# Layer-1 attention, local rounds: the window is kept by a multiplication on VectorE in place of mask matmuls on TensorE

## The reference

```
def local_gqa_attn(x, wq, wk, wv, wo):
    q, k, v = split_heads(x @ wq, 16), split_heads(x @ wk, 4), split_heads(x @ wv, 4)
    q, k = qk_norm(rope(q, BASE_L)), qk_norm(rope(k, BASE_L))
    diff = i[:, None] - i[None, :]
    mask = (diff >= 0) & (diff < 32)
    return merge_heads(sdpa(q, k, v, mask)) @ wo
```

## Time and profile before

| | us |
|---|---|
| median of 3 runs (lowest, highest) | 2619.33 (2613.45, 2625.76) |
| profiled execution | 2615.01 |
| its span | 2613.3 |
| busy: TensorE, VectorE, ScalarE, GpSimd | 2304.5, 1548.6, 1233.7, 953.9 |
| mean granted TensorE clock | 0.933 |

### The profile page before, as it was taken

The page is one execution under the profiler, slowest core; times in us unless marked ns, Lnnn a source line. Parts: engine busy times, 40 slices in busy tenths (PEclk is TensorE's granted clock), DMA queues, the critical chain, the costliest instruction groups (busy, mean ns, idle before and its releaser), DMA issues. The chain is left out here.

```text
span 2613.3 us, 41691 instructions
## 1 busy us (share of the span) xinstructions
PE 2304.5 (88%) x15308; PEld 1392.4 (53%) x15308; DVE 1548.6 (59%) x3383; ACT 1233.7 (47%) x1733; POOL 953.9 (37%) x925
## 2 busy tenths in 40 slices
PE   5999999999999999756999995699999989937586
PEld 2555565556555655445888883334344444524464
DVE  4676757766777577543666667445555445356534
ACT  2555536553655454312333331577877655613241
POOL 0777757775777577610000002223223211000001
PEclk9999999999999999965999997699999988968798
DMA  2000000000000000020000000000000000020001
GB/s 70 1 1 1 1 1 1 1 1 1 1 1 1 1 1 1 1 61 1 0 0 0 0 1 6 1 1 1 1 1 1 1 1 1 2 75 0 0 1 32
DMA packets 35462, 18.03 MB, mean 7 GB/s; under 512 B 15323, under 2 KB 33125, under 8 KB 35301
## 3 DMA queue, kind: packets, MB, share of 16 engines
q1 hardware_dynamic: 35300, 15.86, 2.4%
HBM read 13.76 MB, written 2.10 MB: 6 GB/s over the span
## 5 line engine op out<-in xcount | busy, mean ns | idle before, releaser
L311 POOL TENSOR_TENSOR a_first<-a_first,a_ring 128x512 f32<-128x512 f32 (+3 forms) x352 | 559.9, 1591 | 141.9 <-ACT a_ring L556 106.6
L1576 ACT ACTIVATE g_probsT<-g_s_ps 128x1024 f32<-128x1024 f32 (+2 forms) x448 | 381.8, 868 | 150.3 <-PE g_s_ps L1460 86.6
L556 ACT ACTIVATE a_ring<-a_st 128x768 f32<-128x768 f32 (+1 forms) x256 | 234.8, 917 | 262.8 <-PE a_st L463 262.8
L478 PE MATMUL a_o_ps<-a_ring,a_v 128*64 128x512 f32 (+3 forms) x1280 | 249.2, 485 | 3.2 <-POOL a_ring L293 2.2
L1485 PE MATMUL g_o_ps<-g_probsT,g_values 128*32 128x512 f32 (+5 forms) x2688 | 231.8, 423 | 20.9 <-ACT g_probsT L1576 16.8
L645 DVE RECIPROCAL a_row_inv<-a_row_inv 128x512 f32<-128x512 f32 x64 | 213.7, 3341 | 16.8 <-ACT a_row_inv L544 16.8
L1045 ACT ACTIVATE m_silu<-m_up,m_bias 128x512 f32<-128x512 f32 x160 | 110.1, 688 | 238.8 <-PE m_up L1012 238.8
L1012 PE MATMUL m_up<-m_xT_hi,m_w_hl 128*128 x640 | 211.9, 402 | 7.1 <-DVE m_glu L1061 4.3
L623 DVE TENSOR_REDUCE a_part_max<-a_mx 128x2 f32<-128x1024 f32 x128 | 156.5, 1223 | 103.1 <-PE a_mx L434 99.6
L1460 PE MATMUL g_s_ps<-g_qT,g_kT 64*128 64x512 f32 (+3 forms) x896 | 208.0, 463 | 10.3 <-ACT g_probsT L1576 9.1
L1343 POOL TENSOR_SCALAR_AFFINE_SELECT g_probsT<-g_probsT 128x512 f32<-128x512 f32 x128 | 88.2, 689 | 271.9 <-ACT g_probsT L1576 271.5
(11 more groups left out here) (285 smaller groups left out, 4156.4 us busy)
## 6 DMA issues: line engine op xcount, KB each, us to landing
m_w<-in_L_ffn_rw SPq DMA_DIRECT2D x2, 1024.0 KB, 8.3
s_w<-in_L_ffn_w SPq DMA_DIRECT2D x1, 2048.0 KB, 10.6
s_w<-in_L_ffn_w SPq DMA_DIRECT2D x4, 512.0 KB, 10.4
out_x<-x SPq DMA_DIRECT2D x4, 512.0 KB, 3.2
m_w<-in_L_ffn_rw SPq DMA_DIRECT2D x2, 512.0 KB, 7.6
x<-in_L_attn_x SPq DMA_DIRECT2D x1, 512.0 KB, 4.2
a_outT<-in_L_attn_w_q SPq DMA_DIRECT2D x1, 512.0 KB, 5.0
a_outT<-in_L_attn_w_k SPq DMA_DIRECT2D x1, 512.0 KB, 5.7
```

Of the source, the lines that this page charges most:

```text
L311: pool.tensor_tensor(total[:, h, q:q + w], total[:, h, q:q + w], probs_of(n, u)[:, h, off:off + w], ALU.add).then_inc(added, 1)
L478: last = pe.matmul(o_ps[rows_of(h), first_q:first_q + w], v_half[n // 4 % 2][:, j, head:head + A_HD], probs_of(n, u)[:, h, off:off + w], s ...
L556: act.activation(probs_of(n, u)[:, :, 0:w], st_ps[u % 2][:, :, 0:w], ACT.Exp).then_inc(exp_done, 1)
L1576: act.activation(out, src.rearrange("p k (j n) -> p k j n", j=at_once), ACT.Exp, scale=float(HD) ** -0.5).then_inc(exp_done, 1)
```

## The change

The two mask matmuls of each local step go, and with them `mask_window`, its staging tile, its load and its cast at the start of the kernel. The exponentials are taken of unmasked scores. A tile `keeps` of ones and zeros, [128, 160] float32, is loaded with the stage's weights. VectorE multiplies each step's probabilities in place by it (`keep_window`, one instruction of 640 elements to a partition), at the head of its step, after the step's exponentials; the weighing waits for this product (`window_kept`) instead of `exp_done`.

```diff
--- before.py
+++ after.py
@@ -1225,6 +1225,7 @@
         cos, sin = both("cos", [P, NB, HD // 2]), both("sin", [P, NB, HD // 2])
         w_up = sb("w_up", [LAT, 2 * KV * HD])
         rows_of = sb("rows_of", [P, 2])
+        keeps = sb("keeps", [P, LOCAL_W])
         normed = sb("normed", [P, NB, D])
         normedT = sb("normedT", [P, SEQ])
         qk = sb("qk", [P, NB, QK])
@@ -1254,6 +1255,7 @@
         turned_ready, high_kept, slots_ready = sem("turned_ready"), sem("high_kept"), sem("slots_ready")
         x_filled, x_read_act, x_read_dve = sem("x_filled"), sem("x_read_act"), sem("x_read_dve")
         scored, exp_done, cut, pv_done, o_kept = (sem(n) for n in ("scored", "exp_done", "cut", "pv_done", "o_kept"))
+        window_kept = sem("window_kept")
 
         heads = QK // HD
         as_pairs = lambda t: t[:].rearrange("p t (h n two) -> p t h n two", h=heads, two=2)
@@ -1286,7 +1288,7 @@
             else:
                 eng.wait_ge(x_read_dve, READS_DVE[k])
 
-        LOADS = 16
+        LOADS = 17
 
         with nc.Block() as block:
             @block.sync
@@ -1298,6 +1300,7 @@
                     sp.dma_start(norm_w[layer][:], g.inputs["L1_attn_" + nw].rearrange("(p a) -> p a", a=1)).then_inc(loaded, 16)
                     if layer == 0:
                         sp.dma_start(rows_of[:], g.inputs["c_rows_of"]).then_inc(loaded, 16)
+                        sp.dma_start(keeps[:], g.inputs["c_keeps"]).then_inc(loaded, 16)
                         sp.dma_start(w_in[1][:, D + 32:D + 64], g.inputs["L1_attn_l_wv"]).then_inc(loaded, 16)
                         sp.dma_start(w_up[:, 0:32], g.inputs["L1_attn_g_k_up"]).then_inc(loaded, 16)
                         sp.dma_start(w_up[:, 32:64], g.inputs["L1_attn_g_v_up"]).then_inc(loaded, 16)
@@ -1459,12 +1462,6 @@
                         out = s_ps[u % 2][:, i * HALF:i * HALF + at_once * (e - a)]
                         last = pe.matmul(out, kT[r % 2][s // 2][rows, kb * P:(kb + 1) * P], qT[r % 2][rows, j:j + at_once, a:e],
                                          start=True, stop=True, skip_group_check=True)
-                    for i in range(2) if is_local(r) else ():
-                        width = e - a
-                        out = s_ps[u % 2][:, i * HALF:i * HALF + at_once * width]
-                        keeps = g.mask_window[:, 0:width].unsqueeze(1).to_broadcast([P, at_once, width])
-                        last = pe.matmul(out.rearrange("p (j n) -> p j n", j=at_once), g.ident_bf[:], keeps, start=False,
-                                         stop=True, skip_group_check=True)
                     last.then_inc(scored, 1)
 
                 def weigh(r, n, c):
@@ -1472,7 +1469,9 @@
                     s, kb = n // NB, key_block(r, n)
                     cols = query_cols(r, kb)
                     a, e = cols[c]
-                    if is_local(r) or c:
+                    if is_local(r):
+                        pe.wait_ge(window_kept, steps_up_to(r - BATCH, n))
+                    elif c:
                         pe.wait_ge(exp_done, UNITS_UP_TO[r, n])
                     else:
                         pe.wait_ge(cut, steps_up_to(r, n))
@@ -1635,6 +1634,14 @@
                     dve.wait_ge(pv_done, steps_up_to(x, h * NB + last_of_half(x, c)))
                     dve.tensor_copy(outT[h % 2][:, cols_of(c)], o_ps[:, cols_of(c)]).then_inc(o_kept, 1)
 
+                def keep_window(r, n):
+
+                    width = min(LOCAL_W, SEQ - n % NB * P)
+                    probs = probsT[(r * STEPS + n) % 3][:, :, :, 0:width]
+                    dve.wait_ge(exp_done, UNITS_UP_TO[r, n])
+                    dve.tensor_tensor(probs, probs, keeps[:, 0:width].unsqueeze(1).unsqueeze(1).to_broadcast([P, 2, 2, width]),
+                                      ALU.mult).then_inc(window_kept, 1)
+
                 def scale_weights(layer):
                     width = 192 if layer else 160
                     dve.tensor_scalar(w_in[layer][:, 0:width], w_in[layer][:, 0:width], norm_w[layer][:], None,
@@ -1726,6 +1733,8 @@
                     norm_parts = first_norm(x) if x < BATCH else []
                     ends = residual(r - 1) if r > BATCH else []
                     for n in range(STEPS):
+                        if BATCH <= r < ROUNDS:
+                            keep_window(r, n)
                         for kept in outputs_kept_at(r, n):
                             keep_output(*kept)
                         for k in uses_at(r, n):
@@ -2254,8 +2263,8 @@
         "c_iota": np.arange(E_ROUTED, dtype=np.float32),
 
         "c_mask_kq": np.where(i[:, None] > i[None, :], -1e30, 0.0).astype(np.float32),
-        "c_mask_window": np.where((q - k >= 0) & (q - k < WINDOW), 0.0, -1e30).astype(np.float32),
         "c_rows_of": np.stack([i // SLOT % 2 == c for c in range(2)], axis=1).astype(np.float32),
+        "c_keeps": ((q - k >= 0) & (q - k < WINDOW)).astype(np.float32),
         "c_rope_g": rotation(1e6),
         "c_rope_l": rotation(1e4),
         "c_mask_qk": np.where(i[None, :] > i[:, None], -1e30, 0.0).astype(np.float32),
@@ -2278,18 +2287,16 @@
         g.ident_bf = sb("ident_bf", [P, P], BF16)
         g.minus_half = sb("minus_half", [P, NB])
         g.mask_kq = sb("mask_kq", [P, P], BF16)
-        g.mask_window = sb("mask_window", [P, LOCAL_W], BF16)
         first_ctx = ctx.enter_context(ExitStack())
         g.mask_wide = first_ctx.enter_context(nc.sbuf_tensor("mask_wide", [P, HALF], F32))
-        staged = [first_ctx.enter_context(nc.sbuf_tensor(f"staged{i}", [P, LOCAL_W], F32)) for i in range(2)]
+        staged = first_ctx.enter_context(nc.sbuf_tensor("staged", [P, P], F32))
         const_loaded = ctx.enter_context(nc.semaphore("const_loaded"))
         with nc.Block() as block:
             @block.sync
             def _(sp):
                 sp.dma_start(g.ident[:], g.inputs["c_ident"]).then_inc(const_loaded, 16)
                 sp.dma_start(g.mask_wide[:, HALF - P:HALF], g.inputs["c_mask_qk"]).then_inc(const_loaded, 16)
-                sp.dma_start(staged[0][:, 0:P], g.inputs["c_mask_kq"]).then_inc(const_loaded, 16)
-                sp.dma_start(staged[1][:], g.inputs["c_mask_window"]).then_inc(const_loaded, 16)
+                sp.dma_start(staged[:], g.inputs["c_mask_kq"]).then_inc(const_loaded, 16)
 
             @block.gpsimd
             def _(pool):
@@ -2298,10 +2305,9 @@
 
             @block.vector
             def _(dve):
-                dve.wait_ge(const_loaded, 4 * 16)
+                dve.wait_ge(const_loaded, 3 * 16)
                 dve.tensor_copy(g.ident_bf[:], g.ident[:])
-                dve.tensor_copy(g.mask_kq[:], staged[0][:, 0:P])
-                dve.tensor_copy(g.mask_window[:], staged[1][:])
+                dve.tensor_copy(g.mask_kq[:], staged[:])
         attention_layer0(nc, g)
         first_ctx.close()
         mixture_layer0(nc, g)
```

## The result

The changed kernel takes 2671.65 us, the median of its runs (2665.28 to 2672.8). The kernel before, run beside it, takes 2622.55 us (2613.45 to 2626.91). The ratio is 1.0191, interval 1.0164 to 1.0219: 49 us slower, where 30 were forecast. The sign was right and the size was not: the time lies at the upper end of the range (2672).

What follows compares the result with a forecast made beforehand. TensorE bounds the local stage (busy 222 of 239 us), VectorE one stretch in three rounds. Terms -3.3 + 10.5 + 18.3 - 6 + 12 - 0.6 - 0.5 = +30 take 2615.0 to 2645, forecast median 2649, range 2624 to 2672.

Steps and rivals of the forecast that it cites:

- The multiplication: VectorE, once in each of 128 local steps: 0.82 us alone, about 103 us in all; 1.5 to 2 beside GpSimd.
- Steps 13 to 19: Rotation on VectorE in rounds 4 to 6: four multiplications, GpSimd contention and a last multiplication, +6.1 each, +18.3 us.
- ScalarE's wait for g_turned: Sign to look for: this wait, some 6.4 us three times before the change, would become longer.
- Steps 0 to 2: Rounds 4 to 6: VectorE's order, including GpSimd's root, takes 8.6 us against 5.1: +3.5 each, +10.5.
- Steps 20 to 25: Rounds 4 to 6, after the stall at clock 0.50: steps of 1.47 us against 1.91, -2 each, -6.
- The residual: Steps 26 to 29 of rounds 5, 6 and 7: VectorE's order takes 10.5 us; +3.6, +3.6, +4.8, together +12.
- The ordinary steps at full clock, steps 3 to 12: Rounds 4 to 6: 16.8 us against 17.9, so -1.1 each, -3.3.
- The loop: Ordinary steps: weighing, fill, bank copy, exponentials and multiplication take 3.31 us over two steps, 1.65 each against 1.72.
- Rival (c): Clock stays low in most of the local stage: 0.3 us a step in 50 steps, +15 to +20 more, 2667; chance 0.10.
- the 47 us upper end of what goes: Two mask matmuls in each of 128 local steps, 0.37 us of TensorE: at most 47 us, if nothing else were late.
- Rival (a): Local stage: three probability tiles let multiplications run late, only sums count, 233 under 239; about 2619 us; chance 0.14.
- Rival (b): TensorE's slots come back: some 105 local steps give 0.37 each, -39 with +18 kept, 2598 us; chance 0.06.

Runs made afterwards that it cites:

- GpSimd's select: Kernel before without mask matmuls, weighing two steps behind, GpSimd cutting the window with two affine selects per step: 2647.33 us, ratio 1.0127.
- the other execution: The changed kernel itself, unaltered, run and profiled again: 2668.06 us, ratio 1.0189 to the kernel before.
- the first experiment: Kernel before without the mask matmuls and with nothing in their place, window left out: 2599.83 us, ratio 0.9944.

## Why the prediction was right and wrong

**The multiplication: right.** 0.82 alone, forecast 0.82. Beside GpSimd's products it took 1.89 and 2.17, forecast "1.5 to 2".

**Steps 13 to 19: the size was right, the mechanism in the main.** Forecast +6.1 a round, measured +6.2 in steps 14 to 20, in all three rounds and in both executions. The timeline of round 5, to be held against the earlier trace rows:

```profile
2166.27 0.82 DVE L1673 TENSOR_TENSOR g_part<-g_qk,g_cos 128x640 f32<-128x640 f32 x1 [0.47 <-ACT g_values L1554]
...
2168.83 1.89 DVE L1642 TENSOR_TENSOR g_probsT<-g_probsT,g_keeps 128x640 f32<-128x640 f32 x1
...
2170.77 0.48 PE L1484 MATMUL g_o_ps<-g_probsT,g_values 128*32 128x160 f32 x8 [3.53 <-DVE g_probsT L1642]
...
2175.64 1.99 POOL L1339 TENSOR_TENSOR g_turned<-g_part 128x640 f32<-128x640 f32 x1 [5.61 <-DVE g_ssq L1682]
...
2176.15 2.17 DVE L1642 TENSOR_TENSOR g_probsT<-g_probsT,g_keeps 128x640 f32<-128x640 f32 x1
...
2185.66 0.72 ACT L1561 ACTIVATE g_k_slots<-g_turned 128x256 fp32r<-128x256 f32 x2 [3.22 <-DVE g_turned L1701]
...
2186.42 0.76 PE L1484 MATMUL g_o_ps<-g_probsT,g_values 128*32 128x160 f32 x8 [1.41 <-DVE g_probsT L1642]
...
2187.01 0.82 DVE L1642 TENSOR_TENSOR g_probsT<-g_probsT,g_keeps 128x640 f32<-128x640 f32 x1 [0.64 <-ACT g_probsT L1575]
...
2188.72 0.76 PE L1484 MATMUL g_o_ps<-g_probsT,g_values 128*32 128x128 f32 x16
```

From the rotation's start to ScalarE's start are 19.39 us, 14.88 before: +4.5 for the forecast's 3.3 + 0.5 + 1.4 = 5.2. Behind that point came +1.7, where 0.86 was forecast for one multiplication ahead of the weighing. It isn't the one named: the weighing at 2188.72 has no wait, since the multiplication at 2187.01 ended before TensorE, at 1.2 GHz, had done its fill and scores. The errors of -0.7 and +0.8 cancel, so that the total agrees this well is luck. The Trainium skill, SBUF — State Buffer, "Who interferes with whom", says that VectorE and GpSimd lock a shared pair of ports for a whole instruction; 0.82 alone against 1.89 and 2.17 agrees with it, and so does GpSimd's select at 1.61 for 0.74.

**ScalarE's wait for g_turned: the sign was wrong.** It was to become longer and fell from 6.4 to 3.2 at most. The rotation ends later, but ScalarE comes to it later still, since it waits for scores that TensorE gives late. The wait list names a wait by who comes last; the delay of 4.5 us shows only in the start times.

**Steps 0 to 2: right.** +3.5 forecast, steps 0 to 4 are +2.6, +3.3 and +3.3. The wait for GpSimd's root is the one forecast; beside VectorE the root took 2.15, not 1.65. In round 7, which prepares no input, the same steps are -0.1. (In the other execution, where they ran at 1.2 GHz, they took 11.6 us against 8.5.)

**Steps 20 to 25: right in two rounds.** -1.7 and -1.9 for -2. In round 6 of the kernel before the clock was back sooner (7 us low, not 14; 8.2 us for the steps, against 10.6 and 10.8), so +0.8.

**The residual: the number came, its reason only in part.** Steps 26 to 31 of rounds 5 and 6 are +3.8 and +3.6, where +3.6 was forecast for steps 26 to 29 (these alone: +3.1). But round 4 has no residual, was to give -0.6, and gave +3.3: at the low clock steps 26 to 29 take TensorE 2.30 each, with a bank to fill in each of them. With the residual they took 10.0 and with TensorE alone 9.2, so here both bounds lie close together, and at that clock most of the cost would have been there without any of VectorE's work. The forecast's reason holds by itself too: in the other execution the four steps took 9.5 us in round 6, with the residual, and 6.9 in round 4, without it, both mostly at full clock. In the first experiment, without a multiplication, steps 26 to 31 of round 5 are 13.6. In round 7 the six steps are +4.7 and the four +3.4 (forecast +4.8 for the four).

**The ordinary steps at full clock, steps 3 to 12: right.** The loop was forecast at 1.65 and is 1.60; steps 5 to 13 took 15.6 to 16.0 against 16.4 where the clock was mostly full.

**The step that failed is the clock, the one thing put into a rival.** The sum took full clock outside steps 20 to 25. Score to score, the four rounds grew by 53 us (237.2 to 290.4) where the sum had 31. Measured against the same steps at full clock, steps 5 to 13 are +6.8 in round 4 and +3.7 in round 5 (against 15.9), steps 26 to 31 are +3.5 in round 4 (against 9.9 in the other execution). With the +2.8 of steps 21 to 25 in round 6 (+0.8 for -2) that is 17 of the 22 us. Most of the other 5 lies in round 7, where the runs don't part the clock from VectorE's share. Rival (c) named it, 0.10, and two things were wrong in it. First, its chance: "against it: where VectorE is the bound the clock costs nothing" counts on VectorE being the bound, and in ordinary steps at 1.2 GHz it isn't. Second, its price: it stretched only the 1.07 us of TensorE work inside the loop, 0.3 a step. TensorE's whole step has to be stretched, and then it, not the loop, is the longest: 0.57 + 0.69 + 1.04 = 2.30, 0.65 over the forecast's 1.65. Low and full clock have different bounds, and each has to be worked out by itself. A step without a fill at the low clock stood in the rows, and one with a fill could have been worked out from it. That the rival's 2667 lies within 5 us of the measured time is luck: fewer steps than its 50 ran low, and each cost twice its price.

**What was not in the prediction at all:** that the removed matmuls had a use. The prediction read the low clock with TensorE busy 8.00 of 8 us as something that follows a stall. That such a stretch ends sooner with the masks in was shown only by taking them out (27, 27 and 17 us low, instead of 14, 14 and 7) and by putting such work back (0.65, 0.78, 0.84). Hence also the 47 us upper end of what goes: even with nothing in their place, 16 is all.

Rival (a), that VectorE's order gives way because three tiles let it run late, was rejected on "TensorE asks for the weighing one step after the scores". Weighing two steps behind tests that: some 25 us come back, and about as many stay. It was half right as a mechanism and would have needed an edit that the change doesn't make. Rival (b) had the sum change sign at a multiplication under 0.45 us. Half the multiplication takes 0.49 alone, where the prediction's sum gives some +3; measured were +30 over before. So the slope isn't refuted, but the sum doesn't change sign at 0.45.

**What stays open.** What it is in the mask matmuls that brings the clock back sooner. What VectorE's order would cost at full clock throughout: the 15 to 17 us above are read by stretches, and no run has that order at full clock. That GpSimd's cuts would do better if moved from the rotation's steps wasn't tried.

## What to carry to other kernels

Before taking cheap work off TensorE, ask whether the granted clock hangs on it. Where the clock has been at its lower level in a stretch with TensorE busy throughout, price the rest of the stage at both levels, with the bound worked out anew at each: the work of the other engines keeps its length (the multiplication 0.82, the exponentials 0.70), TensorE's own step goes from 1.34 to 2.30. Work moved to an engine with idle time is to be placed by step and not by sum: VectorE had 125 idle us for 103 us of work and it cost 42, some 25 of them through the clock, while the same multiplication in the steps where it had room, and with one more step of distance to its reader, made the kernel 18 us faster.

## What the runs showed of the hardware that was not expected

TensorE ran at 1.2 GHz while busy without a gap: 20.00 of 20 us in one window, inside 72 us at 0.50 in all (63.3 of them busy). It was executing scores, weighings and bank fills, all fp32. With the two bf16 mask matmuls a step among them, as before, the low stretch around the stall of 5.5 us lasted 14 us, and without them 27; with the masks and the multiplication one of 34 us occurred (30.85 of them busy). How that is decided the runs don't show.

The same program had its low stretches in other rounds in another execution (round 4's steps 5 to 13: 22.7 and 15.6 us), while the medians, 2671.65 and 2668.06, agree. One profile gives the kinds of step, and not which round has them.
